# A two-layer graph kernel: the second layer's owner masks made on ScalarE instead of VectorE

## The reference

```
h = node_features @ W.T + b_W
a1, a2 = (a_vec[:D_OUT], a_vec[D_OUT:])
e = (h @ a1)[:, None] + (h @ a2)[None, :] + b_a[0]
e = jnp.where(e > 0, e, 0.2 * e)
scores = jnp.where(adjacency_matrix > 0, e, jnp.float32(NEG_INF))
attention = jax.nn.softmax(scores, axis=1)
h_prime = attention @ h
```

## Time and profile before

| what | value |
|---|---|
| median of 3 runs | 1683.23 us (1680.87 to 1688.4) |
| the profiled execution | 1679.12 us |
| its span | 1677.3 us |
| busy PE / DVE / ACT / POOL | 1167.8 / 1170.4 / 735.8 / 1147.5 us |

### The profile page before, as it was taken

The page is one execution under the profiler, slowest core; times in us unless marked ns, Lnnn a source line. Parts: engine busy times, 40 slices in busy tenths (PEclk is TensorE's granted clock), DMA queues, the critical chain, the costliest instruction groups (busy, mean ns, idle before and its releaser), DMA issues.

```text
span 1677.3 us, 22627 instructions
## 1 busy us (share of the span) xinstructions
PE 1167.8 (70%) x6317; PEld 923.8 (55%) x6317; DVE 1170.4 (70%) x4201; ACT 735.8 (44%) x2594; POOL 1147.5 (68%) x1170
## 2 busy tenths in 40 slices
PE   5867677777677867767556556677667777676665
PEld 3544344454454544445455456667666677676654
DVE  5886688888887988888757346665666666666544
ACT  3542455656556555555665423232332323333233
POOL 1224777777767777777777177777777777777775
PEclk9998788888888898898767768777777777777778
DMA  9999999999999999998222122222222222222222
GB/s 354 419 373 359 406 408 404 406 408 406 405 390 384 405 400 404 395 389 336 60 56 57 29 55 57 59 57 57 59 58 58 58 58 58 57 58 57 58 59 48
DMA packets 108396, 361.69 MB, mean 216 GB/s; under 512 B 24421, under 2 KB 57576, under 8 KB 75496
## 3 DMA queue, kind: packets, MB, share of 16 engines
q1 hardware_dynamic: 55272, 277.05, 41.2%
q0 software_dynamic: 35840, 74.62, 17.4%
q10 hardware_dynamic: 17152, 8.52, 1.9%
HBM read 347.38 MB, written 12.72 MB: 215 GB/s over the span
## 4 chain that ended last, share of the span: by engine, by line
DMA 30%; POOL 29%; PE 13%; issue 11%; DVE 3%; ACT 2%; POOLq 0%; ACTq 0%; DVEq 0%
DMA arena<-in_adj_dram 28%; POOL arena L547 15%; POOL arena L542 10%; POOL arena L955 4%; PE ps L999 4%; PE ps L1030 3%; PE ps L587 3%; PE ps L505 2%; DMA arena<-tab,idx_all 1%; PE ps L563 1%; PE ps L574 1%; DVE arena L678 0%; DVE negm L680 0%; ACT prod L1122 0%; PE ps L376 0%
## 5 line engine op out<-in xcount | busy, mean ns | idle before, releaser
L955 POOL DMA_INDIRECT arena<-tab,idx_all x576 | 569.6, 989 | 204.7 <-issue 167.9
L999 PE MATMUL ps<-arena,fold 128*128 128x512 fp8e4 x1024 | 302.5, 428 | 182.4 <-DMA arena<-in_adj_dram 181.1
L547 POOL DMA_INDIRECT arena<-tab,idx_all x320 | 324.2, 1013 | 97.6 <-issue 97.6
L542 POOL DMA_INDIRECT arena<-tab,idx_all x224 | 214.8, 959 | 101.0 <-issue 66.2
L999 PEld LDWEIGHTS ps<-arena,fold 128*128 128x128 bf16 x1024 | 89.9, 102 | 347.8 <-DMA arena<-in_adj_dram 252.4
L1122 ACT ACTIVATE prod<-prod,arena 128x128 f32<-128x128 f32 x576 | 221.8, 387 | 35.1 <-DVE prod L1335 35.1
L563 PE MATMUL ps<-ident,arena 128*128 128x128 f32 x704 | 146.2, 383 | 117.3 <-DMA arena<-tab,idx_all 117.3
L563 PEld LDWEIGHTS ps<-ident,arena 128*128 128x128 f32 x704 | 130.1, 280 | 122.8 <-DMA arena<-tab,idx_all 122.8
L617 ACT ACTIVATE arena<-arena,negm 128x517 f32<-128x517 f32 (+1 forms) x64 | 56.8, 887 | 282.0 <-DVE negm L681 282.0
L587 PE MATMUL ps<-arena,diag 128*128 128x130 f32 x640 | 114.3, 340 | 60.7 <-issue 57.4
L1333 DVE TENSOR_TENSOR prod<-arena 128x768 f32<-128x768 f32 x64 | 61.3, 958 | 132.5 <-DMA arena<-tab,idx_all 132.5
(11 more groups left out here) (197 smaller groups left out, 2281.7 us busy)
## 6 DMA issues: line engine op xcount, KB each, us to landing
arena<-in_adj_dram SPq DMA_DIRECT2D x256, 1024.0 KB, 16.7
arena<-tab,idx_all POOLq DMA_INDIRECT x1120, 2.6
tab<-arena ACTq DMA_DIRECT2D x16, 260.0 KB, 14.1
tab<-tw ACTq DMA_DIRECT2D x32, 130.0 KB, 10.0
res<-in_x_dram SPq DMA_DIRECT2D x8, 512.0 KB, 6.0
out_dram<-arena SPq DMA_DIRECT2D x64, 64.0 KB, 1.6
prod<-in_L_gnn_Wq_dram SPq DMA_DIRECT2D x1, 64.0 KB
prod<-in_L_gnn_Wk_dram SPq DMA_DIRECT2D x1, 64.0 KB
```

Of the source, the lines that this page charges most:

```text
L542: pool.indirect_dma_start(out=GS[h % 2][:, c, :], out_offset=None, in_=tab1, in_offset=bass.IndirectOffsetOnAxis(ap=idx_all[:, at, slot:sl ...
L547: pool.indirect_dma_start(out=GO[q][:, s, :], out_offset=None, in_=tab1, in_offset=bass.IndirectOffsetOnAxis(ap=idx_all[:, t, s:s + 1], ax ...
L955: pool.indirect_dma_start(out=G[q][:, s, :], out_offset=None, in_=tab0, in_offset=bass.IndirectOffsetOnAxis(ap=idx_all[:, t, s:s + 1], axi ...
L999: last = nc.tensor.matmul(keys_ps[t % 2], fold[:, PIECE_BITS * f + b, :], ring8[m % RING][:, b * WORDS:(b + 1) * WORDS], start=False, stop ...
```

## The change

The three instructions for a tile move from VectorE to ScalarE. The slots of a node lie around a centre: with the count of its spilled neighbours `spill1` and their end, `end1` now holds minus the centre, and `spill1` is made into a threshold. ScalarE takes the absolute distance of each slot (Abs), a rectified line of it that is zero inside and at least 2^113 outside (`m`, now subtracted from the scores), and a rectified line of that which is one inside and zero outside (`r`). Each waits for the one before. In the second layer's loop the three stand after `own_weights(t)`, for tile t + 10 as before. In the hand-over one tile is made in each of iterations 59 to 68 instead of two in each of 59 to 63; TensorE's owner rows move from two tiles in each of 60 to 64 to one in each of 60 to 69, ScalarE's two copies of them from 62 and 64 to 64 and 68, and VectorE's `select1_vector` from 63 and 65 to 65 and 69.

```diff
@@ -80,6 +80,7 @@
     CODE, ID, OFF, REC = D, D + S, D + S + 1, D + S + 2
     EPS, COS_EPS, LEAK, KEEP = 1e-5, 1e-4, 0.2, 0.5
     FAR = 1e38
+    OUT = float(1 << 113)
     DENSE_FAR = 3e38
     RING, PIECE_BITS = 6, 4
     PIECE, PIECES = PIECE_BITS * WORDS, BITS // PIECE_BITS
@@ -477,27 +478,38 @@
                                                  ALU.is_lt))
                 if SPAN[u][0]:
                     link(nc.vector.tensor_scalar(ends[:, :, u], ends[:, :, u], -float(P * SPAN[u][0]), None, ALU.add))
+
             link.wait(link.n)
+            link(nc.vector.scalar_tensor_tensor(out=end1[:, :], in0=spill1[:, :], scalar=0.5, in1=end1[:, :],
+                                                op0=ALU.mult, op1=ALU.subtract))
+            link(nc.vector.tensor_scalar(end1[:, :], end1[:, :], 0.5, None, ALU.add))
+            nc.vector.tensor_scalar(spill1[:, :], spill1[:, :], -0.5 * OUT, 0.5 * OUT, ALU.mult,
+                                    ALU.add).then_inc(s_n, 1)
 
         def rest_of_offsets1_vector(dve):
             dve.wait_ge(s_E, T)
             nc.vector.tensor_copy(owner[:, 3 * QT:T, OFF], off_ps[:, 3 * QT:T]).then_inc(s_took, 1)
             dve.wait_ge(s_took, PAIRS - LEAD + 2)
 
-        def masks1_vector(dve, link, t):
+        def masks1_scalar(act, t):
+
             first, n = span(t)
             r, m = R1[t % 4][:, 0:n * P], mask[t % (AT1 + 2)][:, 0:n * P]
+            if t == 0:
+                act.wait_ge(s_n, PAIRS + 2)
             if t >= 4:
-                dve.wait_ge(s_part, t - 3)
-            link(nc.vector.tensor_scalar(r, iota1[:, 0:n * P], float(P * first), owner[:, t, OFF:OFF + 1], ALU.add, ALU.is_ge))
-            nc.vector.scalar_tensor_tensor(out=r, in0=iota1[:, 0:n * P], scalar=end1[:, t:t + 1], in1=r,
-                                           op0=ALU.is_lt, op1=ALU.mult).then_inc(s_R1, 1)
-            dve.wait_ge(s_R1, t + 1)
-            link.add(nc.vector.tensor_scalar(m, r, -1.0, FAR, ALU.add, ALU.mult))
+                act.wait_ge(s_part, t - 3)
+            if t >= AT1 + 2:
+                act.wait_ge(s_taken, 2 * (t - AT1 - 1))
+            nc.scalar.activation(r, iota1[:, 0:n * P], ACT.Abs, bias=end1[:, t:t + 1]).then_inc(s_R1, 1)
+            act.wait_ge(s_R1, 3 * t + 1)
+            nc.scalar.activation(m, r, ACT.Relu, bias=spill1[:, t:t + 1], scale=OUT).then_inc(s_R1, 1)
+            act.wait_ge(s_R1, 3 * t + 2)
+            nc.scalar.activation(r, m, ACT.Relu, bias=1.0, scale=-1.0).then_inc(s_R1, 1)
 
         def owners1_tensor(pe, t):
             u, (first, n) = t % QT, span(t)
-            pe.wait_ge(s_R1, t + 1)
+            pe.wait_ge(s_R1, 3 * t + 3)
             if u == 0 and t:
                 pe.wait_ge(s_copied1, t // QT)
             for c in range(first, first + n):
@@ -628,6 +640,8 @@
                     copy_weights(t - 1)
                 if t < T:
                     own_weights(t)
+                if t + AT1 < T:
+                    masks1_scalar(act, t + AT1)
                 q = (t + 5) // QT
                 if t % QT == 3 and 2 <= q < NQ:
                     copy_owners1_scalar(act, q)
@@ -660,6 +674,7 @@
                 s1 = s1_all[:, t:t + 1]
                 m = mask[t % (AT1 + 2)]
                 dve.wait_ge(s_T, t + 1)
+                dve.wait_ge(s_R1, 3 * t + 2)
                 if t >= 2:
                     dve.wait_ge(s_tr1, t - 1)
                     dve.wait_ge(s_dg1, t - 1)
@@ -669,7 +684,7 @@
                     if w > 0:
                         a = K1 + 4 * b * P
                         last = nc.vector.scalar_tensor_tensor(out=sc[p][:, a:a + w], in0=T_ps[b][:, 0:w], scalar=s1,
-                                                              in1=m[:, 4 * b * P:4 * b * P + w], op0=ALU.add, op1=ALU.add)
+                                                              in1=m[:, 4 * b * P:4 * b * P + w], op0=ALU.add, op1=ALU.subtract)
                         last.then_inc(s_taken, 1 if n > 4 else 2)
                 dve.wait_ge(s_taken, 2 * t + 2)
                 dve.wait_ge(s_gm[q], 16 * K1 * (t // GR + 1))
@@ -683,8 +698,6 @@
                     finish(t - 2)
                 if t % QT == 0 and 2 <= t // QT + 1 < NQ:
                     select1_vector(dve, link, t // QT + 1)
-                if t + AT1 < T:
-                    masks1_vector(dve, link, t + AT1)
             finish(T - 2)
             finish(T - 1)
 
@@ -1053,9 +1066,8 @@
                         folds(scan, 0, PIECES // 2)
                     if t == 57:
                         offsets1_tensor(pe)
-                    if 60 <= t < 60 + AT1 // 2:
-                        owners1_tensor(pe, 2 * (t - 60))
-                        owners1_tensor(pe, 2 * (t - 60) + 1)
+                    if 60 <= t < 60 + AT1:
+                        owners1_tensor(pe, t - 60)
                     if t == T:
                         pe.wait_ge(s_miss, 1)
                         nc.tensor.matmul(keys_ps[0][0:1, 0:P], st[:, 4:5], ident[:, :], start=True,
@@ -1180,8 +1192,10 @@
                         weights(t - 2)
                     if t % 2 == 0 and 0 <= t - 8 < T:
                         second.scalar_h(act, (t - 8) // 2)
-                    if t in (62, 64):
-                        copy_owners1_scalar(act, (t - 62) // 2)
+                    if t in (64, 68):
+                        copy_owners1_scalar(act, (t - 64) // QT)
+                    if 59 <= t < 59 + AT1:
+                        masks1_scalar(act, t - 59)
                 either(act, rows_scalar, lists_scalar)
 
             @block.vector
@@ -1412,11 +1426,8 @@
                         offsets1_vector(dve, link)
                     if t == 63:
                         rest_of_offsets1_vector(dve)
-                    if 59 <= t < 59 + AT1 // 2:
-                        masks1_vector(dve, link, 2 * (t - 59))
-                        masks1_vector(dve, link, 2 * (t - 59) + 1)
-                    if t in (63, 65):
-                        select1_vector(dve, link, (t - 63) // 2)
+                    if t in (65, 69):
+                        select1_vector(dve, link, (t - 65) // QT)
                     if t == T - 2:
 
                         link.wait(link.n)
```

## The result

| | before | after |
|---|---|---|
| median of 4 runs each | 1682.05 us (1680.59 to 1688.4) | 1666.45 us (1664.98 to 1669.61) |
| span of the profiled execution | 1677.3 us | 1663.2 us |
| second layer: first gather starts | 959.43 us | 966.74 us |
| second layer: last gather starts | 1663.06 us | 1648.93 us |
| from the one to the other | 703.6 us | 682.2 us |

The ratio of the times is 0.9909, 95% interval 0.9892 to 0.9925. The spans split without a rest: the first gather comes 7.3 us later, the stretch of gathers is 21.4 us shorter.

What follows compares the result with a forecast made beforehand. GpSimd's gathers and their issue were taken to pace the second layer. 1679.1 - 16.6 (gathers) + 9.4 (hand-over) = 1671.9 us, said as 1676 us since the median is 4.1 us higher; range 1670 to 1682, 8 in 10 1664 to 1689.

Steps and rivals of the forecast that it cites:

- What bounds the kernel: Second layer from 959.4 us: GpSimd sets the pace, a gather of about 0.95 us and 0.30 us of issue.
- So a gather has a step near its end that waits for L496: Second layer: 51 long gathers wait near their end for the mask's last instruction; their excess is 16.6 us.
- These cost nothing: Second layer: a gather beside the mask instructions L492 and L493 takes 0.95 us, so they don't delay it.
- The other 30 long ones ... stay: Second layer: 30 long gathers with no L496 beside them, the longest 1.51 us, stay after the change.
- part 1: Second layer's gathers: 16.6 us less, with bounds of 13.5 and 24 us.
- first rival: Gathers gain more, the hand-over loses less: -20 + 6 = -14 us, 1669 us; chance 0.25.
- ScalarE's masks at no cost in the loop: Second layer's loop: three instructions, 2.9 us a wide tile, fit in ScalarE's wait for TensorE's transposes; cost 0.
- The hand-over, +9.4 us: Before the second layer: 15.5 us more, less 6.1; first gather 9.4 us later, bounds 5 and 15 us.
- the earlier start: In the hand-over: owner rows' copy about 3 us earlier, at 924.0, and the last diagonals at 938.3.
- within 0.5%: Outcome in which the whole time differs by no more than 0.5% (8.4 us); chance 0.46.
- Gathers that don't gain because the following instructions move into L496's place: Second layer: any busy VectorE holds gathers, so none get faster; +9 to +12 us, 1694 us; chance 0.12.
- ScalarE as the bound of the loop: Second layer's loop at copy L610: masks make ScalarE too slow; 1 us beyond gives +25, 1708 us; chance 0.05.

Runs made afterwards that it cites:

- the first experiment: Kernel before with its third mask instruction given two inputs, still on VectorE; 2078.54 us, 0.9982 of before.
- the kernel with the masks first: Changed kernel with ScalarE's masks ahead of `own_weights(t)` instead of behind; 1671.81 us, 0.9922 of before.
- the first two experiments: Before with a two-input third mask instruction, 2078.54 us; changed kernel with the three old masks again on VectorE as extra work, 2086.19 us.

## Why the prediction was right, and where it was wrong

- **What bounds the kernel.** Right: the time went where the gathers went, and the stretch's 21.4 us are the gathers' 21.3 us. The idle time between them did not move.
- **"So a gather has a step near its end that waits for L496"** was wrong for these gathers. Their wait begins at the gather's start, and is for the end of L493. A late step that waits for L496's kind exists, but it ends 0.12 us after that instruction, and beside L493 it is never what ends last. "The 0.22 us after L496's end each time" held in 39 gathers and was 0.35 to 0.36 us in the 12 of the narrow tiles, so that the trace of before could have told. That this term came out is luck: the change takes L493 away too, the 51 gathers counted beside L496 are the 51 under L493, and their 16.6 us are the same 16.6 us. A change that had removed L496 alone would have been forecast at -16.6 us and by these counts brought next to nothing; in the first experiment, without L496, the gathers took 551.7 us.
- **"These cost nothing"**, of L492 and L493, was wrong too. In the earlier trace rows L492 begins at 1229.05, 0.03 us behind the gather's start at 1229.02, and L493 at 1229.69; neither was running when the gather started, and L492 was over 0.31 us before the gather's end, too early for the late step. Where L492 had begun 0.1 us before the start, before's trace has the one delay of 0.4 us. The Trainium skill, "SBUF — State Buffer", section "Who interferes with whom", has the rule that fits the runs: a VectorE instruction with two SBUF inputs contends with a GpSimd instruction that reads SBUF. The traces agree by the counts above (51 of 51 under L493), with an indirect gather as such an instruction; and they agree with the page that a reduction does not contend. The prediction weighed only the part on one-input instructions, and that part, too, is borne out: by the 13 gathers that started under L674 and the 15 that ended 0.12 us after it.
- **"The other 30 long ones ... stay"** was the mis-sized term of part 1: -16.6 us stood for -21.4. They had the same cause with other instructions, and 18 were left. The select's went from 14 (3.7 us) to 2 (0.6 us), and two single ones under L492 and L496 went with the masks (0.8 us); the leaky rectifier's stayed (9 and 9). The rest of the 4.8 us, some 1 us, is in gathers under 1.0 us. The first rival had this, "long gathers make the next ones fall at odd moments". That it is phase, the moment at which a gather's start meets an instruction, is supported by the kernel with the masks first, where the same select costs 2.8 us; why the phase came out well in the one order was not tested.
- **ScalarE's masks at no cost in the loop.** Right: 2.70 us a tile for 2.9 reckoned, and two places for them with one time. ScalarE's wait for the transposes did not shrink to the forecast 0.5 us a tile, though: 119.4 us in 42 waits are 2.8 us each. A good part of the masks fell in another wait, that for VectorE's maximum, which went from 282.0 to 216.4 us. A wait that the prediction did not name came up: TensorE now waits for ScalarE's masks, 91.5 us in 16 waits from 900 us on; in the loop this holds no gather up.
- **The hand-over, +9.4 us**, was measured at +7.3. Its later steps were right: 26.5 us forecast from the last diagonals to the last rows, 26.3 us in the trace. The term too small was the earlier start: the owner rows' copy came at 921.54 and not 924.0, and so the diagonals ended 1.7 us before the forecast's 938.3. The 8 passes took 1.88 us, against 4.44 for 20.
- **The sum.** -16.6 + 9.4 = -7.2 us; measured -21.4 + 7.3 = -14.1 us. That is the first rival's -20 + 6 and its 1669 us, against 1666.45 measured. The forecast's own 1676 us is 9.6 us high: 6.9 us by the two terms, the rest since the median of the runs lay 1.5 us above the profiled one after, not 4.1. The time is outside the forecast's own range of 1670 to 1682 and inside the wide one, 1664 to 1689. The direction was right; "within 0.5%", to which the prediction gave the most (0.46), did not come.
- **The rivals that would have been slower.** Gathers that don't gain because the following instructions move into L496's place were not seen: what stays has an input in PSUM, is a maximum, or meets no more starts than before, but for L654 and L656 (7 for 5). ScalarE as the bound of the loop was not seen either: GpSimd's idle time before L554 is issue (68.0 us) and the one wait for the first layer's last rows (43.8 us), so it never waited for TensorE's sums.

Open: what an unchanged hand-over with the loop's masks on ScalarE would take (an estimate from the traces, 7.3 us under the time after, 1659 us), and whether masks on ScalarE slow the loop on a late chip. The kernels with them stood at 1.01 to 1.02 of before in the first and third set, and in the second at 1.00 to 1.02 by medians of 2 or 4 runs; the first experiment, without them, stood at 0.998. The changed kernel itself was not run on such a chip.

## What to carry to other kernels

An instruction that ends a fixed time before another may only be the neighbour of the one that is waited for: look at what was running when the longer one started, look for cases in which the neighbour has another length (the narrow tiles here), and count both the hits and the misses of each kind of instruction. Where GpSimd's gathers set the pace, a VectorE instruction is priced by what it does to the gathers, not by its own length; moving the ones with two SBUF inputs to an engine that waits anyway pays even where that engine is slower. Such a move wins only what the way into the loop does not take: here a third of the gain went into ScalarE's work in the hand-over, so the first portion's place deserves a sum of its own.

## What the runs showed of the hardware

- A gather (0.947 us undisturbed, 0.30 us of issue behind it) that starts during a VectorE instruction with two SBUF inputs ends 0.81 to 0.82 us after that instruction's end: L493 51 of 51, L519 11 of 11, L678 8 of 8 in before; 42 of 42, 38 of 38, 32 of 32 in the experiments under L493's kind. From a lead of 0.09 us on all were delayed; with 0.05 to 0.08 us some were and some were not. An instruction with two SBUF inputs that begins during the gather does not delay it (none of 74 in before).
- A one-input instruction from SBUF to SBUF (L674) does it too, 13 of 13. It also delays a gather if it begins later: begun 0.22 to 0.47 us after the start, it holds the gather until 0.12 us after its own end, if that is later than the gather's own (L674 15 of 15; L492's kind 20 in before, by at most 0.04 us, and 7 and 6 in the first two experiments, by 0.20 to 0.25 us). Begun 0.54 us or more after the start, L674 delayed none of 12, and lasted longer itself (0.73 instead of 0.56 us in 10 of them).
- With one of two inputs in PSUM there is no delay (L671 none in 23, L686 none in 44), nor with a maximum (L680 none in 9, L695 none in 3). Three more ScalarE instructions a tile lengthened no gather (526.5 us beside 526.8).
- The kernel before took 1677 to 1688 us in two sets and 1986 to 2088 us in the three on other chips. In the kernels profiled on these the adjacency stream moved mostly 270 to 350 GB/s, where it moves mostly 365 to 420 GB/s in the profile of after, and GpSimd's issue did not pace the second layer.
